# First mixture of experts: the third shared tile's low part between numbering and slots, two routed tiles' rows loaded together, the first of them transposed behind products

## What is computed

```python
xf = x.reshape(-1, Cc)                                   # normalised x, 2048 x 256
logits = jax.nn.relu(xf @ Wr1 + br1) @ Wr2 + br2
gates = jax.nn.softmax(logits, axis=-1)
tg, ti = jax.lax.top_k(gates, K)                         # K = 2 of E = 8 experts
tg = jax.nn.softmax(tg / K, axis=-1)
out = jax.nn.silu(xf @ Ws1 + bs1) @ Ws2 + bs2            # the shared expert, all tokens
for e in range(E):
    h = jax.nn.silu(xf @ We1[e] + be1[e]) @ We2[e] + be2[e]
    w = jnp.sum(tg * (ti == e), axis=-1)
    out = out + w[:, None] * h
```

## Time and profile before

| | us |
|---|---|
| median of three runs | 916.01 |
| lowest and highest run | 909.1 and 922.09 |
| the profiled execution's own time | 911.56 |
| its span | 909.8 |

### The profile page before, as it was taken

The page is one execution under the profiler, slowest core; times in us unless marked ns, Lnnn a source line. Parts: engine busy times, 40 slices in busy tenths (PEclk is TensorE's granted clock), DMA queues, the critical chain, the costliest instruction groups (busy, mean ns, idle before and its releaser), DMA issues. The chain is left out here.

```text
span 909.8 us, 17895 instructions
## 1 busy us (share of the span) xinstructions
PE 833.0 (92%) x6127; PEld 772.3 (85%) x6127; DVE 668.2 (73%) x1359; ACT 486.5 (53%) x1022; POOL 257.6 (28%) x211
## 2 busy tenths in 40 slices
PE   8988999997889999999999999977999687979977
PEld 6876899996579999999999999945988656969867
DVE  4974899997685457888888879857787677656647
ACT  3643333332475566777777768642555451635643
POOL 8410332232005520233334323220222104402530
PEclk9989999999898999999999999997999888999999
DMA  8990000000403257677777677451000052414325
GB/s 307 302 278 0 2 1 0 1 1 1 151 1 135 93 176 284 232 231 231 230 230 228 217 224 249 132 154 49 2 0 1 17 182 83 139 58 116 107 72 184
DMA packets 60067, 115.93 MB, mean 127 GB/s; under 512 B 8482, under 2 KB 45956, under 8 KB 53220
## 3 DMA queue, kind: packets, MB, share of 16 engines
q1 hardware_dynamic: 48420, 97.48, 32.1%
q0 software_dynamic: 9408, 15.53, 7.0%
q10 hardware_dynamic: 2176, 2.10, 0.7%
HBM read 84.29 MB, written 30.79 MB: 126 GB/s over the span
## 5 line engine op out<-in xcount | busy, mean ns | idle before, releaser
L143 PE MATMUL e_ps_h<-e_xh,e_w1h 128*128 128x256 f32 (+1 forms) x496 | 141.8, 286 | 5.6 <-issue 5.6
L144 PE MATMUL e_ps_h<-e_xl,e_w1h 128*128 128x256 f32 (+1 forms) x496 | 139.2, 281 | 0.0
L145 PE MATMUL e_ps_h<-e_xh,e_w1l 128*128 128x256 f32 (+1 forms) x496 | 138.9, 280 | 0.0
L1991 POOL DMA_INDIRECT accumulated<-m_yo,m_token x39 | 83.0, 2127 | 189.1 <-ACT m_yo L2131 161.1
L143 PE MATMUL e_ps_o<-e_w2h,e_hh 128*128 128x256 f32 x440 | 122.3, 278 | 0.0
L894 POOL TENSOR_TENSOR at_pr<-at_pr,at_inv 128x1168 f32<-128x1168 f32 (+2 forms) x48 | 58.8, 1239 | 223.9 <-DVE at_inv L826 223.9
L145 PE MATMUL e_ps_o<-e_w2h,e_hl 128*128 128x256 f32 x440 | 121.9, 277 | 0.0
L144 PE MATMUL e_ps_o<-e_w2l,e_hh 128*128 128x256 f32 x440 | 121.9, 277 | 0.0
L2111 ACT ACTIVATE e_hf<-e_ps_h,e_b1s 128x256 f32<-128x256 f32 (+1 forms) x248 | 98.2, 447 | 42.0 <-PE e_ps_h L145 41.7
L143 PEld LDWEIGHTS e_ps_h<-e_xh,e_w1h 128*128 128x128 f32 x496 | 94.9, 191 | 5.8 <-issue 5.8
L144 PEld LDWEIGHTS e_ps_h<-e_xl,e_w1h 128*128 128x128 f32 x496 | 95.0, 192 | 0.0
(11 more groups left out here) (427 smaller groups left out, 2331.7 us busy)
## 6 DMA issues: line engine op xcount, KB each, us to landing
e_w1s<-in_m_w SPq DMA_DIRECT2D x24, 1024.0 KB, 4.8
e_w2s<-in_m_w SPq DMA_DIRECT2D x24, 1024.0 KB, 6.9
slots_in<-zero SPq DMA_DIRECT2D x20, 258.0 KB, 8.7
e_xin<-slots_in SPq DMA_DIRECT2D x16, 258.0 KB
last_slots_in<-zero SPq DMA_DIRECT2D x14, 258.0 KB, 7.9
d_xin<-last_slots_in SPq DMA_DIRECT2D x10, 258.0 KB, 2.7
d_results<-last_results SPq DMA_DIRECT2D x10, 256.0 KB, 5.1
as_wk<-in_a_wk SPq DMA_DIRECT2D x2, 1024.0 KB, 9.0
```

Source lines behind the costliest of these rows:

```text
L143: nc.tensor.matmul(out, lh, rh, start=start, stop=False)
L144: nc.tensor.matmul(out, lh, rl, start=False, stop=False)
L145: return nc.tensor.matmul(out, ll, rh, start=False, stop=stop)
L1991: nc.gpsimd.indirect_dma_start(out=g.acc[a], out_offset=bass.IndirectOffsetOnAxis(ap=token[:, n, a:a + 1], axis=0), in_=yo[:, q, a, :], in ...
```

## The change

Four edits, all in `experts`:

1. VectorE's low_x(2), which stood at the head of step 1 and so behind all of `router.slots`, stands between `router.number` and `router.slots`.
2. SyncE loads the rows of tiles 8 and 9 one behind the other as soon as the scatter has landed; step 9 loads no rows any more. Ahead of `early.load` stands a new wait for low_x(7).
3. TensorE's transpose(8) stands behind m1(7) instead of ahead of it. m2(6) follows.
4. ScalarE's high_x(8) stands behind hh(7), and VectorE's token and gate copies and low_x(8) behind hl(7), instead of ahead of them.

No arithmetic is added or removed. The diff:

```diff
--- before.py
+++ after.py
@@ -2005,14 +2005,21 @@
                 e = expert(sp, j, False)
                 wait(sp, s_w1l, unit(j) - 1)
                 load_w1(e, unit(j), 1 - q)
-                wait(sp, s_xlo, j - 1)
                 if static and j == S:
                     for half in m.s_sc:
                         sp.wait_ge(half, 16 * TOPK * NT // 2)
-                if rows_of(j) == 1:
+                if static and j == S:
+                    for i in range(2):
+                        rows = g.xs[i * ST:(i + 1) * ST, :].rearrange("(a p) d -> p a d", p=P)
+                        sp.dma_start(xin[:, (j + i) % 2], rows).then_inc(s_xl[(j + i) % 2], 16)
+                elif static and j == S + 1:
+                    pass
+                elif rows_of(j) == 1:
+                    wait(sp, s_xlo, j - 1)
                     r0 = PAIRS * ST + (j - FIRST) * P
                     sp.dma_start(xin[:, q, 0, :], g.xs[r0:r0 + P, :]).then_inc(s_xl[q], 16)
                 else:
+                    wait(sp, s_xlo, j - 1)
                     rows = g.xs.rearrange("(j a p) d -> j p a d", p=P, a=ROWS)
                     rows = rows[j - S] if static else rows[bass.ds(j - S, 1)].rearrange("j p a d -> p (j a) d")
                     sp.dma_start(xin[:, q], rows).then_inc(s_xl[q], 16)
@@ -2028,6 +2035,7 @@
         sp.dma_start(b2s[:], w["b2"].rearrange("(a e) d -> a e d", a=1).to_broadcast([P, NE, D])).then_inc(s_b2, 16)
         sp.wait_ge(router.s_eid, 1)
         step(S, S % 2)
+        wait(sp, s_xlo, S)
         early.load(sp)
         steps(sp, step, S + 1, J + 1, (S + 3, FIRST - 1))
 
@@ -2035,7 +2043,7 @@
         def make(shared):
             def step(j, q):
                 static = isinstance(j, int)
-                if not static or j + 1 < J:
+                def transpose():
                     direct = static and j + 1 < S
                     if direct:
                         pe.wait_ge(router.s_xn, ROWS * (j + 2))
@@ -2050,6 +2058,9 @@
                             src = m.xn[:, ROWS * (j + 1) + a, ks] if direct else xin[:, 1 - q, a, ks]
                             last = nc.tensor.transpose(ps_x[:, 1 - q, k, a * P:(a + 1) * P], src, g.ident[:])
                     last.then_inc(s_tr, 1)
+
+                if not static or j + 1 < J and j != S - 1:
+                    transpose()
                 if not static or 0 <= j < J:
                     common = is_shared(j, shared)
                     wq = 0 if common else 1 - q
@@ -2064,6 +2075,8 @@
                                 last = product(nc, o, (first(w1h, wq, k, MG * mp + i), first(w1l, wq, k, MG * mp + i)),
                                                (xh[:, q, k, 0:n], xl[:, q, k, 0:n]), k == 0, k == DK - 1)
                         last.then_inc(s_m1, 1)
+                if static and j == S - 1:
+                    transpose()
                 if not static or j >= 1:
                     common = is_shared(j - 1, shared)
                     wq = 0 if common else q
@@ -2097,7 +2110,8 @@
                         if not static or j > S - 1:
                             wait(act, s_m1, MP * j)
                         high_w1(act, unit(j + 1), q)
-                    high_x(act, j + 1, 1 - q)
+                    if not static or j != S - 1:
+                        high_x(act, j + 1, 1 - q)
                 if not static or 0 <= j < J:
                     if static and j == 0:
                         act.wait_ge(s_b1, 16)
@@ -2115,6 +2129,8 @@
                         wait(act, s_m2, j - 1)
                         ms = slice(MG * mp, MG * (mp + 1))
                         nc.scalar.copy(hh[:, q, ms, 0:n], hf[:, ms, 0:n]).then_inc(s_hh, 1)
+                    if static and j == S - 1:
+                        high_x(act, S, 1 - q)
                 if shared and not static or static and 0 <= j - 2 < S:
                     wait(act, s_sx, j - 1)
                     rows = g.acc[0][0:TOK].rearrange("(j a p) d -> j p a d", p=P, a=ROWS)
@@ -2155,22 +2171,30 @@
         def make(shared):
             def step(j, q):
                 static = isinstance(j, int)
+                def routed_x(i, qi):
+                    wait(dve, s_xh, i + 1)
+                    n = i - S
+                    rows = slice(0, rows_of(i))
+                    for dst, col in ((token, TOKEN), (gate, GATE)):
+                        nc.vector.tensor_copy(dst[:, n, rows] if static else dst[:, bass.ds(n, 1), :].rearrange("p n a -> p (n a)"),
+                                              xin[:, qi, rows, col])
+                    low_x(dve, i, qi)
+
                 if not static or j + 1 < J:
                     if not is_shared(j + 1, shared):
                         low_w1(dve, unit(j + 1), q)
-                        wait(dve, s_xh, j + 2)
-                        n = j + 1 - S
-                        rows = slice(0, rows_of(j + 1))
-                        for dst, col in ((token, TOKEN), (gate, GATE)):
-                            nc.vector.tensor_copy(dst[:, n, rows] if static else dst[:, bass.ds(n, 1), :].rearrange("p n a -> p (n a)"),
-                                                  xin[:, 1 - q, rows, col])
-                    low_x(dve, j + 1, 1 - q)
+                        if not static or j != S - 1:
+                            routed_x(j + 1, 1 - q)
+                    elif not static or j != 1:
+                        low_x(dve, j + 1, 1 - q)
                 if not static or 0 <= j < J:
                     w = P * rows_of(j)
                     for mp in range(MP):
                         wait(dve, s_hh, j * MP + mp + 1)
                         ms = slice(MG * mp, MG * (mp + 1))
                         nc.vector.tensor_tensor(hl[:, q, ms, 0:w], hf[:, ms, 0:w], hh[:, q, ms, 0:w], ALU.subtract).then_inc(s_hl, 1)
+                    if static and j == S - 1:
+                        routed_x(S, 1 - q)
                 if not static or 1 <= j <= J:
                     wait(dve, s_m2, j)
                     if static and j == 1:
@@ -2190,6 +2214,7 @@
                         nc.vector.tensor_tensor(x, x, yo[:, 1 - q], ALU.add).then_inc(s_sx, 1)
                 if static and j == 0:
                     router.number(dve, ps_c)
+                    low_x(dve, 2, 0)
                     router.slots(dve)
                 if not static or j + 1 < J:
                     if not is_shared(j + 1, shared):
```

## The result

| | changed | before, in the same comparison |
|---|---|---|
| median of 20 runs each | 910.85 us | 914.78 us |
| lowest and highest | 902.21 and 918.46 us | 906.46 and 922.09 us |
| the profiled execution's own time (span) | 911.55 us (909.8) | 911.56 us (909.8) |

The ratio is 0.9955, with a 95% interval of 0.9935 to 0.9974: 4.1 us faster (2.4 to 5.9), and with 2% as the measure no change. Runs more than 1.5% above the fastest of their kernel count as slow and are left out of every ratio here; with all twenty runs in, the two medians give 0.9957. Two later comparisons of the same two kernels gave 0.9955 (0.9924 to 0.9987) and 0.994 (0.991 to 0.9971). The forecast was 912.6 us and a gain of 3.4 us.

What follows compares the result with a forecast made beforehand. TensorE was taken as the bound, except for a 5.6 us pause before m1(2) on low_x(2). Of 5.75 us gained, a wait of 1.6 to 2.3 before m1(9) leaves 3.4: 912.6 us from the median 916.01, range 904 to 919.

Steps and rivals of the forecast that it cites:

- The 5.75 us of edit 1: At m2(1): with low_x(2) ahead of the slots, TensorE is 5.75 us ahead if the clock stays up.
- The clock behind this pause: Behind the pause before m2(1): even chances of a clock drop costing 2.5 us, swallowed by a later wait.
- one of my own signs of being wrong: Listed as showing the forecast wrong: the granted clock falling behind the pause before m2(1) or before m1(9).
- The 0.61 us on the scatter's side: Slots, first scatter and the whole chain of 32 come 0.61 us later; tile 8's rows load at 331.3.
- Edits 3 and 4, transpose(8) behind m1(7): At transpose(8): a wait of 0 to 0.7 us, without the move 6 us; keeps the gain, earns nothing itself.
- Edit 2: At transpose(9): loading the rows of tiles 8 and 9 together saves between 0 and 0.6 us of a wait.
- What is late next: Before m1(9): VectorE waits for w2 of unit 1, TensorE waits 1.6 to 2.3 us, 3.4 of 5.75 us left.
- The rate of about 358 GB/s: HBM's limit for one core, cited for the full-gain rival: bytes in 2.5 us sooner, m1(9) without a wait.
- The full gain of 5.75 us: Rival, chance 0.12: w2 of unit 1 lands by 345, TensorE's own pace decides at m1(9), 910.3 us.
- A drop of the clock behind m1(9)'s wait: Rival, chance 0.22: the pause before m1(9) drops the clock, 2.5 of 3.4 us given back, gain 0.9, 915.1 us.
- A w2 so late that the change turns into a loss: Rival, chance 0.08: w2 of unit 1 lands at 350.4, m1(9) starts at 357.0, 2.0 us slower, 918.0 us.

Runs made afterwards that it cites:

- a2: The changed kernel run again without modification, beside the kernel before: 911.46 us against 915.25, ratio 0.9955 (0.9924 to 0.9987).
- a3: The changed kernel run a third time without modification, beside the kernel before: 908.99 us against 913.81, ratio 0.994 (0.991 to 0.9971).
- e2: The changed kernel without edit 1, low_x(2) back behind the slots: 914.13 us against 913.26 before, ratio 0.9997.
- e8: e5 with VectorE's hl(1) moved ahead of the last seven instructions of the slots: 911.29 us against 913.81 before, ratio 0.9967.
- e1: The kernel before with edit 1 alone: 918.0 us against 913.26 before, ratio 1.0033 (1.0006 to 1.0059).
- e3: The changed kernel without edit 2, tile 9's rows again loaded behind the early loads and w1 of unit 2: 916.87 us against 913.26 before, ratio 1.0021.
- e6: Changed kernel with early loads behind w1 of unit 2 and w2 of unit 1, and tile 5's store held until behind the scatter: 910.45 us, again 907.85.
- e5: Changed kernel with the nine early loads behind w1 of unit 2 and w2 of unit 1: 910.74 us against 915.25 before, ratio 0.9951.
- e4: Changed kernel with w2 of unit 1 loaded ahead of the scatter's wait: 910.75 us against 913.26 before, ratio 0.9962; again 0.9871, from two runs.

## Why the prediction was right, and which of its terms were not

**The 5.75 us of edit 1: right in kind, 0.3 us too small.** At transpose(4) TensorE is 6.1 us ahead in a2 and in a3 (281.41 - 255.94 = 25.47, against 31.53 before). The pause before m2(1) was 2.11 us there and 2.08 in the first profile, forecast some 2.4: hl(1) starts 17.3 us behind transpose(2) in all three profiles, before 17.5 (273.79 - 256.28), so it comes 0.2 us sooner and not at the same time.

**The clock behind this pause: one of my own signs of being wrong came true, and the size was too large.** The working gave even chances, and yet the list of what would show it wrong named a fall of the granted clock behind either pause. It fell in the first profile and not in a2 and a3. Of the eleven profiles with a pause of some 2 us there (before, e2 and e8 have none), four show the drop: the first of the changed kernel, e1, e3 and the second e6. In all four, and in none of the other seven, step 0 too had run at the low clock; so it doesn't look like a coin thrown at this pause, but why step 0 runs low in some executions the traces don't show. The drop costs 1.6 to 1.7 us, not 2.5. That a later wait swallows it was right for the changed kernel: in the first profile m1(9) waited for low_x(9) all the same. In e6's second profile, where m1(9) doesn't wait, it is not swallowed.

**The 0.61 us on the scatter's side: mis-sized.** The first scatter came 15.96, 15.98 and 16.00 us behind transpose(2), before 15.55: a shift of 0.4 us. What counts more is the length of the scatter, for which the sum has no term. It was 58.4 to 58.9 us in six profiles and 60.1 to 63.4 in the other eight. Both profiles without edit 1 are in the short group. Whether edit 1 itself makes a long scatter more frequent, two profiles can't tell; it stays open.

**Edits 3 and 4, transpose(8) behind m1(7): right.** No wait in the first profile, forecast 0 to 0.7. e1 shows the loss without them and edit 2, 6.29 us of wait where the working said 6, and a clock that I had left out of this term.

**Edit 2: the step that was wrong.** The prediction said that it "saves between 0 and 0.6 us of a wait", because it let tile 9's rows land 3.4 us after their issue, the bound from tile 8's rows. But tile 8's rows have nothing ahead of them in the queue, and tile 9's have 1 MB of early loads and 1 MB of w1. Before, this was hidden, since TensorE came to transpose(9) 5.75 us later. With edit 1 the cover is gone: e3 measured 7.3 us, a wait of 4.34 us, 2.7 us of low clock, and the whole gain lost. The forecast didn't suffer, because the changed kernel has edit 2 and the term stood in the sum at nothing. But whoever had left edit 2 out on my word would have had no gain.

**What is late next: right in kind, too pessimistic in size.** VectorE waits for w2 of unit 1 (4.89 us, forecast 5 to 6), and from high_w2 to the end of low_x(9) it is 356.44 + 0.68 - 350.63 = 6.49 us, forecast 6.5. The load took 8.1 us from its issue (350.63 - 342.56) and in a3 7.4, where I had taken 9.1 from the earlier trace rows. So m1(9) waited 0.99, 1.15 and 0.89 us and not 1.6 to 2.3, and the gain is 3.07, 4.5 and 4.9 us. What tells the three apart is the load of w2 alone: high_w2 starts 91.57, 90.11 and 89.72 us behind transpose(2) (350.63 - 259.06, 351.34 - 261.23, 345.66 - 255.94), and this and the gain add up to 94.6 in each. The clock has no part in it. In the first profile w2 was issued 83.5 us behind transpose(2) where the forecast had 82.1, since the scatter was longer, and its load was 1.0 us shorter than forecast; that the 3.07 lies so near to the 3.4 is luck, two errors that cancel. In a2 and a3 the issue was as forecast (82.0 and 82.3), and the shorter load shows in the gain. So 9.1 us for this load is the term that was mis-sized: 7.4 to 8.1 us were measured in the changed kernel. The measured 4.1 us lies between the three profiles, 0.7 above the forecast. The two views of the DMA's rate in the first profile:

```profile
341.00:347.00 6.00, 6.00 (x54) 6.00 (x54) 1.53 (x3) 0.00 (x0) 0.00 (x0) 1.00 1.00 341
347.00:353.00 6.00, 6.00 (x54) 6.00 (x53) 2.33 (x2) 4.75 (x8) 0.00 (x0) 1.00 1.01 405
```

The engines are full, at 341 and 405 GB/s. The rate of about 358 GB/s, by which one rival went, is no ceiling here. The Trainium skill ("HBM Reference", Specifications (TRN2)) gives about 425 GB/s for a core that streams alone, and the 405, above the 358 and below the 425, agree with that.

**The rivals.** The full gain of 5.75 us is what e5's profile shows (5.64): once w2 lands soon enough, m1(9) doesn't wait and TensorE's own pace decides, as this rival had it. What brought the landing forward there is that the early loads stand behind it, which the rival did not name; the changed kernel doesn't reach it. A drop of the clock behind m1(9)'s wait appeared in none of its three profiles: from 357.26 of the first and from the same place in the others the remainder is 552.5, 552.6 and 552.4 us, as before (552.25). A w2 so late that the change turns into a loss didn't appear. The loss that the experiments found is another one: rows that arrive late, in e1 and e3 and in e4's profile, which the prediction had only as the reason for edits 3 and 4.

**The spread.** transpose(2) itself stood between 255.9 and 262.1 us in the fourteen profiles, and the remainder behind m1(9) took 549.7 to 557.8 us. The change touches neither, and each spread (6 and 8 us) is larger than the term. That is why one profile's span says nothing about a change of 4 us.

## What to carry to other kernels

When an early pause is removed, go through everything that TensorE will now reach that much sooner, and ask of each input where its DMA stands in its queue; the time of a transfer was here not that of its bytes alone but also of what was issued ahead of it. The edits that protect a gain (here the joined loads and the later transpose) were worth nothing without edit 1, and without them edit 1 was worth nothing either, so such edits should be tested by leaving out one at a time. Here that was done for edit 1 and for edit 2, not for edits 3 and 4 by themselves. And compare two traces from a common point just ahead of the change, not by their spans.

## What the runs showed of the hardware that I had not expected

- The same 32 indirect DMAs, two in flight, took from 58.4 to 63.4 us, and 58.4 to 60.4 in three profiles of one and the same kernel. The last of the 32 instructions on GpSimd took 3.02 us in e6's first profile and 2.99 in e8's, and the last but one 2.39 in e4's, where most take 0.97 to 1.5.
- 258 KB of rows landed 2.7 to 3.1 us after their issue with nothing ahead of them, 4.8 to 5.0 us (in a2) with 1 MB just ahead, 7.3 us (e3) with 1 MB just ahead and another ahead of that, and 9.1 us in a3, where the rows of tile 10, issued at 339.77, stand behind 3 MB of weights issued in the 2.6 us before.
- The low clock (1.2 GHz) came in five of fourteen profiles in step 0, behind a pause of 1.19 us (the row at 249.82 above) and the router's small products, and cost 1.6 to 2.8 us. All fourteen have this pause, so the pause alone doesn't decide it. Behind a wait of 1.5 us at transpose(8) it didn't come, behind each of the six waits of 3.5 to 6.3 us there or at transpose(9) it did, at 1.4 to 2.8 us apiece.
